# Windowed attention on one core: a PSUM copy moved from ScalarE to VectorE, and a group of transposes moved between the two halves of the score matmuls

## The chip, the cores and the metric

The kernel runs on one core of a Trainium2 chip. A core has a matmul engine (TensorE, PE in the profile, its weight loads PEld), VectorE (DVE), ScalarE (ACT), GpSimd (POOL) and SyncE (SP), each with its own instruction stream; they meet at semaphores. The metric is the device time of one execution in microseconds (us).

## What is computed

Four blocks follow each other on a tensor of 16 images of 28 x 28 positions and 32 channels. The change lies in the first one, attention inside windows of 7 x 7 positions with 4 heads of 8 channels:

```python
win = win.reshape(-1, WS * WS, C)              # windows of 49 positions
qkv = win @ w_qkv + b_qkv
attn = softmax(einsum('whnd,whmd->whnm', q, k) * scale)
out = einsum('whnm,whmd->whnd', attn, v)
out = out @ w_proj + b_proj                    # x = x + out
```

The others (a convolution with a state-space scan, a triangle product, a gated recurrence) are the same in both kernels.

## The kernel before

The partitions hold 4 groups of 32 channels (`G = 4`, group g of images on partitions 32g to 32g+31), and the columns are cut into `NS = 16` strips of 196, each one row of four windows for every group. Each engine has a function for one stage `s` (`pe_att`, `act_att`, `dve_att`, `pool_att`), and stage s works on three strips at once: it prepares strip s+1 (`nxt`: queries, keys, values), takes the scores and their exponentials of strip s (`cur`), turns the probabilities of strip s-1 and multiplies them with the values (`prv`), and projects strip s-2 (`prv2`). The order of work on each engine is written out by hand; there is no scheduler. The stages from 3 on run in loops of two stages on PE, ACT, DVE and POOL.

In one stage PE does, in this order:

- `transposes(0)`: the probabilities `Pr` of group 0 of strip s-1, four transposes of 113 x 113 (L1167), into one of two PSUM banks that the four groups take by turns (`pair2` and `pair3`, the "ring").
- `scores(0)` and `scores(1)` (L1127): queries times keys, groups 0 and 1, then groups 2 and 3. Each matmul has 32 rows of weights and 64 columns, so it sits in one of eight tiles of the array: the row of tiles is the group, and the column is the half of the output's partitions. A half of the scores is eight matmuls of 196 columns; the line has x32 in the profile, two records for a matmul. Semaphore `s_r` counts the halves.
- `transposes(1)`, then queries and keys of strip s+1 (L1203, L1204) into `banks[4]`, then `transposes(2)` and `transposes(3)`.
- `project()` (L1149) writes the projection into the same `banks[4]`, so it waits until ACT has taken queries and keys from it (`k_r`); it also waits for the attended values `AO` from DVE (`ao_r`).
- values of strip s+1 (L1221), then `av()`: probabilities times values (L1178, x64) and the sums of the softmax (L1186, x16).

ACT takes the four turned groups out of PSUM (`turned_out`, L688, `PT<-pair`), after the second of them `Qw` and `Ks` (L705, L710), then four exponentials (L697), four copies of the values (L729) and the inverse of the sums (L738, L740, tile `den`). Semaphore `ring_r` counts its copies out of the ring.

DVE takes maxima and differences of a half (`shifted`, L1851 and L1857, two each), then `AO` (L1863), then the other half, then the residual `X` (L1880). Between stages it has other small work to do, such as the normalization of a later image.

```python
                shifted(0)
                if prv2:
                    attended()
                shifted(1)
```

Of the kernel before, what the change touches and what calls it, by code (L numbers as in the profile page):

```python
# [14 lines left out]
G = P // C  # L15
# [6 lines left out]
WT = WS * WS  # L22
# [19 lines left out]
def build(nc, a, out):  # L42
    ctx = ExitStack()
    with ctx:
# [164 lines left out]

        qk_d, v_r, s_r, t_r, av_r, pj_r, q_r, k_r, exp_r, ring_r = sems("qk_d v_r s_r t_r av_r pj_r q_r k_r exp_r ring_r")
        xw_r, km_r, max_r, sub_r, sum_r, ln_r, rec_r, ao_r, x1_r, ones_r = sems("xw_r km_r max_r sub_r sum_r ln_r rec_r ao_r x1_r ones_r")


# [428 lines left out]
        def _(eng):  # L644
# [31 lines left out]
            def act_att(s, par, before_output=None):  # L676
                fixed = isinstance(s, int)
                nxt = not fixed or s + 1 < NS
                cur = not fixed or 0 <= s < NS
                prv = not fixed or 1 <= s <= NS  # L680
                np_ = 1 - par
                def turned_out(g):
                    if not prv:
                        return
                    eng.wait_ge(t_r, 4 * (s - 1) + g + 1)
                    if g == 0 and (not fixed or s >= 2):
                        eng.wait_ge(sum_r, s - 1)
                    eng.activation(PT[0:KW, g].rearrange("p a b (o q) -> p (a b o) q", o=2),  # L688
                                   banks[5 + (par + 1 + g) % 2][0:KW, :].rearrange("p (m k) -> p m k", k=WP)[:, :, 0:WT], ACT.Copy).then_inc(ring_r, 1)

                def exponent(g):
                    if not cur:
                        return
                    eng.wait_ge(sub_r, 4 * s + g + 1)
                    if not fixed or s >= 2:
                        eng.wait_ge(t_r, 4 * (s - 2) + g + 1)
                    eng.activation(Pr[:, par, g, :, 0:WT], Ts[:, g, :, :], ACT.Exp).then_inc(exp_r, 1)  # L697

                turned_out(0)
                turned_out(1)  # L700
                if nxt:
                    eng.wait_ge(qk_d, s + 2)
                    if not fixed or s >= 1:
                        eng.wait_ge(s_r, 2 * s)
                    eng.activation(Qw[:, np_, :, 0:WT].rearrange("p w (r c) -> p w r c", r=WS),  # L705
                                   windows(banks[4][:, 0:ST]), ACT.Identity,
                                   bias=vec[:, V_BQS:V_BQS + 1], scale=SCALE).then_inc(q_r, 1)
                    if not fixed or s >= 1:
                        eng.wait_ge(km_r, s)
                    eng.activation(Ks[:, np_].rearrange("p w (r c) -> p w r c", r=WS),  # L710
                                   windows(banks[4][:, ST:2 * ST]), ACT.Identity,
                                   bias=vec[:, V_BK:V_BK + 1]).then_inc(k_r, 1)
                turned_out(2)
                turned_out(3)
                for g in range(G):
                    exponent(g)
                if nxt:
                    eng.wait_ge(v_r, s + 2)
                    if not fixed or s >= 1:
                        eng.wait_ge(av_r, s)  # L720
                    if fixed and s < 0:
                        eng.wait_ge(s_mk2, 3)
                    vb = banks[5 + (par + 1) % 2]
                    for u in range(2):
                        for o in range(2):
                            src = vb[64 * o:64 * o + 64, 0:2 * P].rearrange("p (m e q d) -> p m e q d", m=8, e=2, q=2)[:, :, :, u, :]
                            dst = Vst[64 * u:64 * u + 64, np_, o].rearrange("p v g e n -> p (v g) (e n)")
                            dst = bass.AP(dst.tensor, dst.offset + HD * u, [list(dst.ap[0]), [64, 8], [48, 2], [1, HD]])
                            ins = eng.activation(dst, src, ACT.Copy)  # L729
                        ins.then_inc(ring_r, 1)  # L730

                if fixed and s < 0:
                    evacuated(3, 1)
                if before_output:
                    before_output()
                if prv:
                    eng.wait_ge(sum_r, s)
                    eng.activation(den[:, :], banks[7][:, 256:256 + ST], ACT.Ln).then_inc(ln_r, 1)  # L738
                    eng.wait_ge(ln_r, s)
                    eng.activation(den[:, :], den[:, :], ACT.Exp, scale=-1.0).then_inc(rec_r, 1)  # L740
# [344 lines left out]
        def _(eng):  # L1085
# [18 lines left out]
            def pe_att(s, par, early=None, late=None):  # L1104
# [45 lines left out]


                last = fixed and s == NS
                base = 6 * (s - 1) + 4 - (2 if last else 0)

                def transposes(g):
                    eng.wait_ge(exp_r, 4 * (s - 1) + g + 1)

                    if g == 0:
                        eng.wait_ge(ring_r, base if last else base - 2)
                    elif g == 1:  # L1160
                        eng.wait_ge(ring_r, base)
                    else:
                        eng.wait_ge(ring_r, base + g - 1)
                    bk = banks[5 + (par + 1 + g) % 2]
                    for k in range(4):
                        pg = Pr[0:KW, np_, g, 2 * k:2 * k + 2, :].rearrange("p h k -> p (h k)")[:, 0:KW]
                        ins = eng.transpose(bk[0:KW, P * k:P * k + KW], pg, ident[0:KW, 0:KW])  # L1167
                    ins.then_inc(t_r, 1)

                def av():  # L1170

                    eng.wait_ge(ring_r, base + G)
                    if not fixed or s >= 2:
                        eng.wait_ge(ao_r, s - 1)
                    for w in range(NW):
                        for e in range(2):
                            for g in range(G):
                                ins = eng.matmul(banks[7][C * g:C * g + C, WT * w:WT * w + WT], Vst[:, np_, w % 2, w // 2, g, e, :],  # L1178
                                                 PT[:, g, w // 2, e, WT * (w % 2):WT * (w % 2) + WT],
                                                 start=(e == 0), stop=(e == 1))  # L1180
                    ins.then_inc(av_r, 1)
                    if fixed and s == 1:
                        eng.wait_ge(ones_r, 3)
                    for e in range(2):
                        for g in range(G):
                            ins = eng.matmul(banks[7][C * g:C * g + C, 256:256 + ST], ones[:, e, :], PT[:, g, :, e, :],  # L1186
                                             start=(e == 0), stop=(e == 1))
                    ins.then_inc(sum_r, 1)
# [1 line left out]
                if prv:  # L1190
                    transposes(0)
                scores(0)
                scores(1)
                if prv:
                    transposes(1)
                if nxt:
                    if fixed and s < 1:
                        eng.wait_ge(s_xn, s + 2)
                    if not fixed or s >= 0:
                        eng.wait_ge(k_r, s + 1)  # L1200
                    if not fixed or s >= 3:
                        eng.wait_ge(x1_r, s - 2)
                    eng.matmul(banks[4][:, 0:ST], BD[:, U_Q, :], XN[:, strip(s + 1)], start=True, stop=True)  # L1203
                    eng.matmul(banks[4][:, ST:2 * ST], BD[:, U_K, :], XN[:, strip(s + 1)], start=True, stop=True).then_inc(qk_d, 1)  # L1204
# [11 lines left out]
                if nxt:  # L1216
                    eng.wait_ge(xw_r, s + 2)
                    if prv:
                        eng.wait_ge(ring_r, base + 3)
                    for v in range(NW // 2):  # L1220
                        ins = eng.matmul(banks[5 + (par + 1) % 2][:, P * v:P * v + P],  # L1221
                                         xw[:, np_, 2 * v:2 * v + 2].rearrange("p o k -> p (o k)"),
                                         BD[:, U_V, :], start=True, stop=True)
                    ins.then_inc(v_r, 1)
# [19 lines left out]
            def claim(name, b):  # L1244
# [8 lines left out]
                        eng.wait_ge(a_m, d + 1)  # L1253
                elif place(name, b) >= 2:

                    eng.wait_ge(ring_r, 6 * NS)
                    eng.wait_ge((x1_r, ao_r)[place(name, b) - 2], NS)
                order.append((name, b))

# [458 lines left out]
        def _(eng):  # L1718
# [119 lines left out]
            def dve_att(s, par, before_residual=None):  # L1838
# [21 lines left out]
                def attended():  # L1860
# [2 lines left out]
                    eng.tensor_tensor(windows(AO[:, par, :]), by_window(banks[7][:, 0:ST]),  # L1863
                                      by_window(den[:, :]), ALU.mult).then_inc(ao_r, 1)

                shifted(0)
                if prv2:
                    attended()
# [400 lines left out]
```

## Time and profile before

| what | value |
|---|---|
| median of 3 runs | 429.19 us (427.34 to 432.02) |
| the profiled execution: its own time, and its span | 428.95 us, 426.8 us |
| mean granted TensorE clock | 0.967 |
| attention's stages | about 14 to 123 us of the span |
| one stage in its steady state | 6.40 us |

The span is the time from the first to the last instruction; some 2.15 us of the execution's time lie around it. The row of each stage begins where `transposes(0)` does.

### The profile page before, as it was taken

How to read it: one execution, taken by the hardware profiler on the slowest of the kernel's cores; microseconds unless marked ns; L12 is line 12 of the kernel's file. 1: busy time of each engine (PE TensorE's matmuls, PEld its weight loads, DVE VectorE, ACT ScalarE, POOL GpSimd, SP SyncE). 2: the span in 40 equal slices, each digit the busy share in tenths (PEclk: the TensorE clock that was granted, in tenths of full speed). 3: DMA queues.
4: the chain of work that ended last, by engine and by line, in shares of the span. 5: the costliest groups of instructions: out<-in, count | busy, mean ns of one | idle time of the engine just before them, and what ended most of it. 6: DMA issues, size and time to landing. Idle time of an engine off the chain costs nothing.

```text
span 426.8 us, 11111 instructions
## 1 busy us (share of the span) xinstructions
PE 373.2 (87%) x4065; PEld 256.2 (60%) x4065; DVE 318.9 (75%) x637; ACT 286.2 (67%) x600; POOL 162.3 (38%) x139
## 2 busy tenths in 40 slices
PE   5899999999998798798799776898978979999996
PEld 5677777777754243253354333443963569888885
DVE  3879887788746699899689889995658957555554
ACT  3589899999858676649857764449974354444443
POOL 8314323223103246754954978961632400000000
PEclk9989999999999898899989988999999989999999
DMA  6120000004123353354222222200030001111111
GB/s 162 7 20 8 2 0 1 0 0 98 34 67 93 116 141 119 116 144 119 103 103 102 102 98 97 85 0 0 2 77 2 2 1 23 16 22 22 22 22 27
DMA packets 28671, 23.17 MB, mean 54 GB/s; under 512 B 21105, under 2 KB 22897, under 8 KB 28641
## 3 DMA queue, kind: packets, MB, share of 16 engines
q1 hardware_dynamic: 28244, 22.73, 19.4%
q8 instruction: 18, 0.29, 0.3%
q10 hardware_dynamic: 396, 0.05, 0.1%
q14 instruction: 13, 0.10, 0.1%
HBM read 2.00 MB, written 1.61 MB: 8 GB/s over the span
## 4 chain that ended last, share of the span: by engine, by line
PE 37%; DVE 25%; issue 13%; ACT 9%; POOL 7%; DMA 4%; SPq 3%; DVEq 1%; ACTq 0%; POOLq 0%
PE pair L1671 6%; DVE pair L1966 3%; PE pair L1291 3%; PE pair L1167 3%; DVE Ts L1857 3%; PE pair L1178 3%; DVE stats L1745 3%; PE pair L1127 3%; PE pair L1659 2%; DMA Cs<-BCf 2%; SPq L419 2%; DVE Hs L1978 2%; PE pair L1186 2%; PE pair L1149 2%; PE pair L1279 2%
## 5 line engine op out<-in xcount | busy, mean ns | idle before, releaser
L535 POOL TENSOR_TENSOR hC<-Hs,Cs 128x784 f32<-128x784 f32 x31 | 61.9, 2001 | 47.5 <-DVE Hs L1978 31.6
L503 POOL TENSOR_TENSOR Km<-Ks,mask 128x784 f32<-128x784 f32 x16 | 24.2, 1509 | 69.3 <-ACT Ks L710 69.3
L1344 PE MATMUL pair<-hC,ident 128*128 128x392 f32 x128 | 50.4, 520 | 0.0
L1851 DVE TENSOR_REDUCE mx<-pair 128x8 f32<-128x392 f32 x64 | 32.9, 555 | 17.0 <-PE pair L1127 17.0
L1340 PE MATMUL pair<-BCf,sel 96*128 96x392 bf16 x64 | 22.5, 355 | 19.9 <-DVE Hs L1978 17.6
L1966 DVE TENSOR_TENSOR pair<-DU,pair 128x392 f32<-128x392 f32 x64 | 35.5, 555 | 5.8 <-PE pair L1340 5.3
L1671 PE MATMUL pair<-hst,BD 128*128 128x112 f32 x224 | 37.2, 297 | 2.1 <-DVE Rt L2238 0.4
L1167 PE MATMUL pair<-ident,Pr 113*113 113x113 f32 x256 | 37.1, 279 | 2.1 <-issue 1.2
L1167 PEld LDWEIGHTS pair<-ident,Pr 113*113 113x113 f32 x256 | 31.0, 183 | 12.2 <-issue 11.4
L1978 DVE TENSOR_TENSOR_SCAN Hs<-dA,Hs,pair 128x392 f32<-128x392 f32 x32 | 32.9, 1030 | 3.3
L1671 PEld LDWEIGHTS pair<-hst,BD 128*128 128x128 f32 x224 | 29.6, 192 | 9.1 <-DVE hst L2232 5.2
L1978 DVE TENSOR_TENSOR_SCAN Hs<-dA,pair 128x392 f32<-128x392 f32 x32 | 31.1, 970 | 4.2
L1344 PEld LDWEIGHTS pair<-hC,ident 128*128 128x128 f32 x128 | 25.0, 200 | 15.2 <-issue 5.2
L827 ACT ACTIVATE dA<-DL,Aneg 128x784 f32<-128x784 f32 x32 | 29.1, 941 | 6.8 <-POOL DL L545 5.3
L1659 PE MATMUL pair<-XN,BD 128*128 (+1 forms) x224 | 31.7, 286 | 1.8 <-ACT XN L1048 1.8
L697 ACT ACTIVATE Pr<-Ts 128x392 f32<-128x392 f32 x64 | 31.4, 546 | 2.5 <-DVE Ts L1857 1.9
L1857 DVE TENSOR_TENSOR Ts<-pair,mx 128x392 f32<-128x392 f32 x64 | 32.8, 553 | 0.0
L1340 PEld LDWEIGHTS pair<-BCf,sel 96*128 96x128 bf16 x64 | 6.3, 100 | 43.4 <-issue 37.5
L688 ACT ACTIVATE PT<-pair 113x392 f32<-113x392 f32 x64 | 29.7, 496 | 3.9 <-PE pair L1167 2.9
L1659 PEld LDWEIGHTS pair<-XN,BD 128*128 128x128 f32 x224 | 28.0, 197 | 2.3 <-ACT XN L1048 2.3
L1068 ACT ACTIVATE gates<-pair 128x112 f32<-128x112 f32 x28 | 7.4, 264 | 28.9 <-PE pair L1671 28.9
L2219 DVE SCALAR_TENSOR_TENSOR prods<-gates 128x112 f32<-128x112 f32 x28 | 7.7, 275 | 24.0 <-ACT gates L1068 24.0
(255 smaller groups left out, 851.2 us busy)
## 6 DMA issues: line engine op xcount, KB each, us to landing
Cs<-BCf SPq DMA_DIRECT2D x32, 392.0 KB
SX<-XP SPq DMA_DIRECT2D x48, 112.2 KB
XT<-in_x SPq DMA_DIRECT2D x4, 392.0 KB, 6.4
out<-Os SPq DMA_DIRECT2D x28, 56.0 KB, 1.7
AD<-Aa SPq DMA_DIRECT2D x4, 196.0 KB
NB<-in_L_conv_x_proj_w SPq DMA_DIRECT2D x4, 3.0 KB
DW<-in_L_conv_dw SPq DMA_DIRECT2D x4, 1.1 KB
W<-in_L_conv_w_qkv ACTq DMA_DIRECT2D x1, 48.0 KB
```

Source lines behind the costliest of these rows:

```text
L535: eng.tensor_tensor(hC[:, i % NHC, :], Hs[:, i % NHS, :], Cs[i % NCS][:, :], ALU.mult).then_inc(v_c, 1)
L688: eng.activation(PT[0:KW, g].rearrange("p a b (o q) -> p (a b o) q", o=2), banks[5 + (par + 1 + g) % 2][0:KW, :].rearrange("p (m k) -> p m ...
L697: eng.activation(Pr[:, par, g, :, 0:WT], Ts[:, g, :, :], ACT.Exp).then_inc(exp_r, 1)
L827: eng.activation(dA[:, n % NA, :], DL[:, c % 2, :], ACT.Exp, scale=Aneg[:, n:n + 1]).then_inc(a_da, 1)
L1167: ins = eng.transpose(bk[0:KW, P * k:P * k + KW], pg, ident[0:KW, 0:KW])
L1344: return eng.matmul(STATES[:, h, :], ident[:, :], src[:, columns(h)], start=first, stop=last)
L1659: eng.matmul(zb[k].rearrange("p (b n) -> p b n", b=J), BD[:, U_X + k, :], xt, start=False, stop=False, skip_group_check=True)
L1671: eng.matmul(zb[k], BD[:, U_M + k, :], hst[:, 1 - par, :], start=False, stop=True, skip_group_check=True).then_inc(done, 1)
L1851: eng.tensor_reduce(mx[:, g, :], banks[g][:, 0:392].rearrange("p (m k) -> p m k", k=WT), AX.X, ALU.max).then_inc(max_r, 1)
L1857: eng.tensor_tensor(Ts[:, g, :, :], banks[g][:, 0:392].rearrange("p (m k) -> p m k", k=WT), bcast(mx[:, g, :], 2, WT), ALU.subtract).then_ ...
L1966: eng.tensor_tensor(SPREAD[:, columns(h)], DU[:, c % 2, columns(h)], SPREAD[:, columns(h)], ALU.mult).then_inc(v_b, 1)
L1978: eng.tensor_tensor_scan(Hs[:, i % NHS, columns(h)], dA[:, n % NA, columns(h)], SPREAD[:, columns(h)], h0, ALU.mult, ALU.add).then_inc(v_s, 1)
```

## The change

Group 0's turned probabilities are copied out of PSUM by DVE, as its first work of a stage, ahead of the maxima; the copy has a semaphore of its own, `t0_r`. ACT is left with groups 1 to 3, so `ring_r` counts 5 copies a stage where it counted 6. On PE, `transposes(1)` stands between `scores(0)` and `scores(1)`. The waits follow: `transposes(2)` waits for `t0_r` (its bank is group 0's), `transposes(3)` for ACT's copy of group 1, `av()` for both counters.

```diff
@@ act_att
-                    if g == 0 and (not fixed or s >= 2):
+                    if g == 1 and (not fixed or s >= 2):
                         eng.wait_ge(sum_r, s - 1)
...
-                turned_out(0)
                 turned_out(1)
@@ pe_att
-                base = 6 * (s - 1) + 4 - (2 if last else 0)
+                base = 5 * (s - 1) + 4 - (2 if last else 0)
...
                     elif g == 1:
                         eng.wait_ge(ring_r, base)
+                    elif g == 2:
+                        eng.wait_ge(t0_r, s)
                     else:
-                        eng.wait_ge(ring_r, base + g - 1)
+                        eng.wait_ge(ring_r, base + 1)
...
-                    eng.wait_ge(ring_r, base + G)
+                    eng.wait_ge(t0_r, s)
+                    eng.wait_ge(ring_r, base + 3)
...
                 if prv:
                     transposes(0)
                 scores(0)
-                scores(1)
                 if prv:
                     transposes(1)
+                scores(1)
...
                     if prv:
-                        eng.wait_ge(ring_r, base + 3)
+                        eng.wait_ge(ring_r, base + 2)
@@ dve_att
+                if prv:
+                    eng.wait_ge(t_r, 4 * (s - 1) + 1)
+                    if prv2:
+                        eng.wait_ge(sum_r, s - 1)
+                    eng.tensor_copy(PT[0:KW, 0].rearrange("p a b (o q) -> p (a b o) q", o=2),
+                                    banks[5 + (par + 1) % 2][0:KW, :].rearrange("p (m k) -> p m k", k=WP)[:, :, 0:WT]).then_inc(t0_r, 1)
                 shifted(0)
                 if prv2:
                     attended()
```

On PE, stage 2 before, from `transposes(0)` to the first of `transposes(2)`; `pair0` holds the scores of groups 0 and 1, `pair1` those of 2 and 3, `pair2` has `banks[4]` and one bank of the ring, `pair3` the other one:

```order
L1167 MATMUL pair3<-ident,Pr 113x113 [waits ring_r,exp_r]
L1127 MATMUL pair0<-Km,Qw 64x196 [waits sub_r,km_r,q_r]
L1127 MATMUL pair0<-Km,Qw 64x196 x7
L1127 MATMUL pair1<-Km,Qw 64x196 [waits sub_r]
L1127 MATMUL pair1<-Km,Qw 64x196 x7
L1167 MATMUL pair2<-ident,Pr 113x113 [waits ring_r,exp_r]
L1167 MATMUL pair2<-ident,Pr 113x113 x3
L1203 MATMUL pair2<-XN,BD 128x196 [waits k_r]
```

The same place now:

```order
L1168 MATMUL pair3<-ident,Pr 113x113 [waits ring_r,exp_r]
L1126 MATMUL pair0<-Km,Qw 64x196 [waits sub_r,km_r,q_r]
L1126 MATMUL pair0<-Km,Qw 64x196 x7
L1168 MATMUL pair2<-ident,Pr 113x113 [waits ring_r,exp_r]
L1168 MATMUL pair2<-ident,Pr 113x113 x3
L1126 MATMUL pair1<-Km,Qw 64x196 [waits sub_r]
L1126 MATMUL pair1<-Km,Qw 64x196 x7
L1205 MATMUL pair2<-XN,BD 128x196 [waits k_r]
L1168 MATMUL pair3<-ident,Pr 113x113 [waits t0_r,exp_r]
```

The second group's transposes stand between the two halves of the scores, and the scores of groups 2 and 3 directly ahead of the queries (L1205). On DVE, stage 5 before, after the normalization of an image:

```order
L1764 TENSOR_SCALAR XN<-X,mv,rstd 128x784 [waits s_mv,s_rs]
L1851 TENSOR_REDUCE mx<-pair0 128x8 [waits s_r]
L1857 TENSOR_TENSOR Ts<-pair0,mx 128x392 [waits exp_r,max_r] x2
L1863 TENSOR_TENSOR AO<-pair3,den 128x4x7x7 [waits rec_r]
L1851 TENSOR_REDUCE mx<-pair1 128x8 [waits s_r]
```

And now:

```order
L1767 TENSOR_SCALAR XN<-X,mv,rstd 128x784 [waits s_mv,s_rs]
L1873 COPY PT<-pair2 113x392 [waits sum_r,t_r]
L1854 TENSOR_REDUCE mx<-pair0 128x8 [waits s_r]
L1860 TENSOR_TENSOR Ts<-pair0,mx 128x392 [waits exp_r,max_r] x2
L1866 TENSOR_TENSOR AO<-pair3,den 128x4x7x7 [waits rec_r]
```

The copy stands ahead of the maxima and waits for the transposes of group 0 (`t_r`).

## Rows read from the trace of the kernel before

**Rows 1.** The chain that ended last, by engine and by line (the page).

```profile
PE 37%; DVE 25%; issue 13%; ACT 9%; POOL 7%; DMA 4%; SPq 3%; DVEq 1%; ACTq 0%; POOLq 0%
```

**Rows 2.** Timeline of stage 7: start, duration, engine, line, tiles, idle before.

```profile
60.55 1.08 DVE L1769 TENSOR_TENSOR BD<-W,bd 128x896 f32<-128x896 f32 x1
...
61.01 0.65 PE L1167 MATMUL pair<-ident,Pr 113*113 113x113 f32 x4
...
61.59 0.95 PE L1127 MATMUL pair<-Km,Qw 32*64 32x196 f32 x32
...
62.46 0.47 PEld L1167 LDWEIGHTS pair<-ident,Pr 113*113 113x113 f32 x4 [0.28 <-issue]
62.46 0.65 PE L1167 MATMUL pair<-ident,Pr 113*113 113x113 f32 x4
62.55 1.04 DVE L1851 TENSOR_REDUCE mx<-pair 128x8 f32<-128x392 f32 x2 [0.92 <-PE pair L1127]
62.67 0.97 ACT L688 ACTIVATE PT<-pair 113x392 f32<-113x392 f32 x2
...
62.95 0.51 PE L1203 MATMUL pair<-XN,BD 128*128 x2
...
63.30 0.49 PE L1204 MATMUL pair<-XN,BD 128*128 x2
...
63.63 0.96 PE L1167 MATMUL pair<-ident,Pr 113*113 113x113 f32 x8
63.91 0.43 ACT L705 ACTIVATE Qw<-pair,vec 128x196 f32<-128x196 f32 x1 [0.26 <-PE pair L1204]
64.23 0.42 ACT L710 ACTIVATE Ks<-pair,vec 128x196 f32<-128x196 f32 x1
64.45 0.35 DVE L1863 TENSOR_TENSOR AO<-pair,den 128x196 f32<-128x196 f32 x1
64.54 0.89 ACT L688 ACTIVATE PT<-pair 113x392 f32<-113x392 f32 x2
...
64.93 0.59 PE L1149 MATMUL pair<-AO,BD 128*128 128x196 f32 x2 [0.34 <-DVE AO L1863]
```

**Rows 3.** Windows: busy time of stage 7 (PE, PEld, DVE, ACT, POOL), granted clock.

```profile
61.00:67.40 6.40, 6.06 (x142) 4.98 (x138) 5.09 (x11) 5.94 (x17) 1.81 (x2) 1.00 0.00 0
```

**Rows 4.** Timeline of stage 0, where a wait parts the two halves of the scores.

```profile
15.74 0.54 PEld L1127 LDWEIGHTS pair<-Km,Qw 32*64 32x64 f32 x16 [0.43 <-ACT X L268]
...
16.57 0.60 PE L1203 MATMUL pair<-XN,BD 128*128 128x196 f32 x2
...
17.00 0.49 PE L1204 MATMUL pair<-XN,BD 128*128 128x196 f32 x2
```

**Rows 5.** Timeline of stage 2: the keys and the attended values.

```profile
31.55 0.42 ACT L710 ACTIVATE Ks<-pair,vec 128x196 f32<-128x196 f32 x1
...
31.92 0.35 DVE L1863 TENSOR_TENSOR AO<-pair,den 128x196 f32<-128x196 f32 x1
```

**Rows 6.** Timeline of stage 1, PE.

```profile
22.60 0.88 PE L1167 MATMUL pair<-ident,Pr 113*113 113x113 f32 x4 [0.79 <-ACT Vst L729]
...
23.27 0.88 PE L1203 MATMUL pair<-XN,BD 128*128 128x196 f32 x2
...
24.59 1.73 PE L1167 MATMUL pair<-ident,Pr 113*113 113x113 f32 x8
```

**Rows 7.** Windows: the same stretch of stage 1, columns as in rows 3.

```profile
22.90:26.20 3.30, 3.30 (x16) 3.14 (x14) 3.15 (x7) 2.32 (x6) 0.54 (x1) 0.50 0.22 18
```

**Rows 8.** A DVE copy out of PSUM ahead of the stages (timeline).

```profile
14.34 0.97 DVE L268 COPY X<-pair 128x448 f32<-128x448 f32 x1 [0.77 <-PE pair L1095]
```

**Rows 9.** Waits from 28 to 115 us: total, times, longest.

```profile
DVE mx L1851 <- PE pair L1127: 17.0, 11, 2.0
```

**Rows 10.** Timeline of stage 15, which has no queries and keys.

```profile
113.77 1.95 PE L1167 MATMUL pair<-ident,Pr 113*113 113x113 f32 x12
...
115.75 0.35 DVE L1863 TENSOR_TENSOR AO<-pair,den 128x196 f32<-128x196 f32 x1
```

More of the change, by code:

```diff
@@ L206, in sems @@
             return [sem(n) for n in names.split()]
-        qk_d, v_r, s_r, t_r, av_r, pj_r, q_r, k_r, exp_r, ring_r = sems("qk_d v_r s_r t_r av_r pj_r q_r k_r exp_r ring_r")
+        qk_d, v_r, s_r, t_r, av_r, pj_r, q_r, k_r, exp_r, ring_r, t0_r = sems("qk_d v_r s_r t_r av_r pj_r q_r k_r exp_r ring_r t0_r")
         xw_r, km_r, max_r, sub_r, sum_r, ln_r, rec_r, ao_r, x1_r, ones_r = sems("xw_r km_r max_r sub_r sum_r ln_r rec_r ao_r x1_r ones_r")
@@ L1254, in claim @@
                 elif place(name, b) >= 2:
-                    eng.wait_ge(ring_r, 6 * NS)
+                    eng.wait_ge(ring_r, 5 * NS)
+                    eng.wait_ge(t0_r, NS)
                     eng.wait_ge((x1_r, ao_r)[place(name, b) - 2], NS)
```

## The prediction

> **What bounds the kernel now.** I read three views in this order: the chain that ended last, the timeline of one steady stage, and the windows for the busy time in it. In the chain PE leads with 37%, DVE follows with 25% and ACT has 9% [rows 1]; the reader is to see that work alternates between PE and DVE and that ACT's copies are hardly on it. The timeline of stage 7 shows the loop [rows 2]. PE turns group 0 from 61.01, runs all scores from 61.59; DVE, idle for 0.92 us, begins the maxima of groups 0 and 1 at 62.55, takes two maxima and two differences and then `AO`, done at 64.45 + 0.35 = 64.80; the projection begins at 64.93, and then values, probabilities times values and sums lead to the next `transposes(0)`, one stage of 6.40 us later. So what ends the projection's wait is `AO`. Right behind it is a second path to the same projection: scores, `transposes(1)`, queries (62.95), keys (63.30), ACT's `Qw` (63.91) and `Ks` (done at 64.23 + 0.42 = 64.65). It is 0.15 us early. In stage 2 it is 32.27 - 31.97 = 0.30 us early [rows 5]. I take 0.20 us as the slack of the keys' path in a stage. PE is busy for 6.06 of 6.40 us and ACT for 5.94, so neither can take much more [rows 3].
>
> **The copy on DVE.** DVE gains one copy of 113 x 392 out of PSUM a stage. The trace has no such copy. The nearest rows are the maximum over 392 columns of PSUM, 1.04 us for two that overlap a little, some 0.55 us each [rows 2], and a copy of 128 x 448 out of PSUM with scattered writes, 0.97 us [rows 8]. ACT's own copy of the same tile is 0.97 us for two [rows 2]. I take 0.55 us. It may begin when group 0 is turned, 61.01 + 0.65 = 61.66, and DVE waits for the scores until 62.55 anyway; in stage 7 it has even finished an extra product at 60.55 + 1.08 = 61.63. So it ends near 62.25, and the maxima keep their start. This gap is DVE's wait for the scores, 17.0 us in 11 waits between 28 and 115 us, the longest 2.0 [rows 9]. At 0.97 us the copy would end near 62.65 and put `AO` 0.1 us later; where DVE comes late from its extra work, by up to 0.55 to 0.97 us. I set it at nothing, since the path by way of the keys becomes later still (below), by about 0.75 us a stage. If that cover were gone, a late stage would pay up to 0.55.
>
> **The copy off ACT.** ACT loses 0.45 to 0.5 us a stage, between `den` and the copy of group 1. What follows is `Qw`, and before it ACT already sits idle for 0.26 us, waiting for the keys' matmul [rows 2]. Group 1's copy can't begin before its transposes end, now near 62.42 + 0.65 = 63.07 (below), so it ends near 63.6 as before, ahead of `Qw`: zero on the path.
>
> **The transposes between the halves.** This is the term that counts. Before, both halves of the scores together hold PE from 61.59 to 62.46, 0.87 us [rows 2]. Stage 0 shows what one half alone takes: the weight loads of the second half begin at 15.74, after a wait that parts them from the first, and the query matmul begins at 16.57 [rows 4]. That is 0.83 us for 8 matmuls against 0.87 for 16. The halves lie in different rows of tiles of the array, and run at the same time when they are issued one behind the other. A group of transposes uses 113 rows and columns, so with `transposes(1)` between them the halves are run one after the other, and the second costs its full time again.
>
> Step by step in stage 7: `scores(0)` from 61.59, 0.83 us; `transposes(1)`, 0.58 us (from `transposes(0)` at 61.01 to the scores at 61.59); `scores(1)`, 0.83; and from the first query matmul to the first key matmul 0.43, as in stage 0 behind scores (16.57 to 17.00), where it is 0.35 behind transposes. The keys' matmul then begins at 61.59 + 0.83 + 0.58 + 0.83 + 0.43 = 64.26 in place of 63.30, 0.96 us later. `Qw` and `Ks` follow it at once and end 0.96 us later, at 65.61. The projection needs both `Ks` and `AO`; `AO` stays, so 0.20 us of slack is used up and the projection is 0.76 us later. `transposes(2)` and `(3)` end near 65.55, before it. What stands behind the projection (values, probabilities times values, sums, next `transposes(0)`) moves with it, as do ACT's two last copies. The second half of the maxima comes behind `AO` and still finds its scores done, near 63.8.
>
> Bounds of this term: no less than if a half cost half of the pair, 0.44 us. Then the keys' matmul begins at 61.59 + 0.44 + 0.58 + 0.44 + 0.43 = 63.48, 0.18 later, inside the slack: 0. No more than if each half takes the pair's 0.87 and no slack is left: 1.04 us. I take 0.76, because stage 0 measures the very thing, with the same operands and the query matmul behind it.
>
> The Trainium skill says the same of the array (TensorEngine Tiling (Array Packing), Key Properties): tiles run in parallel, and changing the tiling mode drains the engine. The trace agrees, with 0.28 us of idle weight loading ahead of the transposes after the scores [rows 2]. By its rule of independent tiles alone a half would cost as much as the pair, 0.87 us, an estimate of 1.04 a stage before slack and of 441 us in all.
>
> **How many stages.** Queries and keys are made behind the scores in stages 1 to 14. Stages 2 to 14 are 13: 13 x 0.76 = 9.9 us. Stage 1 has no `AO`, and its path runs through PE: `transposes(1)` wait there for ACT's values and start at 22.60, with the queries at 23.27 [rows 6]. Now `scores(1)` comes behind them, at least 0.83 us. TensorE's granted clock is 0.50 there, the lower of its two levels (1.2 of 2.4 GHz) [rows 7], so it may be up to 1.6; what comes later then leaves the slow stretch, in which eight transposes took 1.73 us instead of 0.96. I take 1.0. Stage 15 has no queries: its 12 transposes, begun at 113.77, are done at 115.72, before `AO` at 116.10 [rows 10], and a second half of scores ahead of the last 8 leaves the projection waiting on `AO` or a copy at nearly the same time: 0, at most 0.2. Stages 16 and 17 have no scores; DVE's copy there lies in a long wait: 0.
>
> Sum: 9.9 + 1.0 = 10.9 us. The profiled execution's 428.95 becomes 439.9, its span 437.7; the median of the runs, 429.19, lies 0.24 above the profiled one and becomes 440.1. I forecast 440.0.
>
> **Rivals.**
>
> *The halves cost only their share* (a half 0.44 us). Then the keys' path stays within its slack, stages 2 to 14 pay nothing and stage 1 about 0.5: 429.7 us. For it: 16 matmuls in eight tiles could have been serial in part. Against it: rows 4, the only place where a half stands alone. Chance 0.06.
>
> *Part of it only.* Stage 0's 0.83 us may hold an unseen wait that a steady stage lacks. With 0.66 us a half the keys' matmul is 0.62 later, 13 x 0.42 + 0.8 = 6.3 us: 435.5. Chance 0.08.
>
> *ACT is the bound, and the change is faster.* ACT is busy for 5.94 of 6.40 us [rows 3], and four copies, a `Qw` and a `Ks` stand in a row between `den` and the projection. If ACT's length set the stage, the 0.49 us taken from it would shorten each stage until PE's 6.06 us bind: 0.34 x 13 = 4.4 us, 424.8. It decides where ACT never waits between `den` and `Ks`. Against it: the 0.26 us that ACT waits for PE before `Qw` [rows 2]. It needs the halves to cost nothing as well. Chance 0.03. The Trainium skill speaks for this side (TensorEngine Tiling (Array Packing), PSUM Bottleneck): once tiling has sped up TensorE the PSUM copies may bind, and both ScalarE and VectorE should take them out. The row on `Qw` says that they don't bind here.
>
> *DVE's copy lands on the path as well.* If it takes 0.97 us and all 13 stages start their maxima 0.5 us late or more, `AO` still ends near 65.3, before the new `Ks` at 65.6; only three or four stages with extra DVE work would pay some 0.3 us each: 441. Were it to cost more than 1.3 us, it would pass the keys: 443 to 445. Chance 0.03.
>
> **How the numbers follow.** The forecast has 0.80, and its own spread (0.6 to 0.95 us a stage, 0.8 to 1.6 in stage 1) is 437.5 to 443. A measurement of this kernel tells about 1%, 4.3 us, from no change. The range reaches down to the partial case and up to each half at the pair's price: 434.5 to 443.5, which leaves out the first and the third rival and part of the last. Slower by over 1% are the forecast, the partial case and the copy on the path, 0.91, less 0.02 for the partial case's lower edge: 0.89. Within 1%: 0.08. Faster: 0.03.
>
> **What would show it.** In the profile of the changed kernel a steady stage should be near 7.15 us long. The score matmuls should come as two groups of x16, 1.4 us apart, each 0.83 us from the next full-array matmul. The projection's wait should end by ACT's `Ks` instead of `AO`. ACT should wait about 1.2 us ahead of `Qw`, and DVE's copy should start right behind group 0's transposes and end before the scores. I am wrong if the query matmul follows the second half after 0.5 us or less, if the projection still waits for `AO`, or if the copy takes over 1 us.

## The result, and the profile after

The changed kernel takes 442.02 us (median of 4 runs, 439.73 to 443.77) beside 430.39 us for the kernel before (4 runs): a ratio of 1.0268, with a 95% interval of 1.0219 to 1.0317. It is slower by 11.6 us. The forecast was 440.0 us, and slower.

The profiled execution took 443.5 us with a span of 441.3 us, one of the longer of the four; the rows below are from it. First the chain that ended last, by engine and by line, from its page:

```profile
PE 42%; DVE 21%; issue 11%; ACT 10%; POOL 7%; DMA 6%; ACTq 1%; SPq 1%; DVEq 1%; POOLq 0%
PE pair L1168 6%; PE pair L1126 6%; PE pair L1674 5%; DVE pair L1975 4%; DMA Cs<-BCf 3%; PE pair L1180 3%; PE pair L1294 3%; PE pair L1188 2%; DVE Hs L1987 2%; DVE stats L1748 2%; PE pair L1148 2%; PE pair L1205 2%; PE pair L1223 2%; POOL hC L535 2%; DMA vec<-in_L_conv_b_qkv 2%
```

PE had 37% of the chain and DVE 25% [rows 1]; now PE has 42 and DVE 21. The transposes (L1168) and the scores (L1126) lead it.

The timeline of stage 7, which answers to [rows 2] (start, duration, engine, line, tiles, idle before):

```profile
67.27 0.65 PE L1168 MATMUL pair<-ident,Pr 113*113 113x113 f32 x4
...
67.85 0.89 PE L1126 MATMUL pair<-Km,Qw 32*64 32x196 f32 x16
67.96 0.57 DVE L1873 COPY PT<-pair 113x392 f32<-113x392 f32 x1 [0.65 <-PE pair L1168]
...
68.67 0.65 PE L1168 MATMUL pair<-ident,Pr 113*113 113x113 f32 x4
68.81 1.04 DVE L1854 TENSOR_REDUCE mx<-pair 128x8 f32<-128x392 f32 x2 [0.28 <-PE pair L1126]
...
69.25 0.89 PE L1126 MATMUL pair<-Km,Qw 32*64 32x196 f32 x16
...
70.07 0.30 PEld L1205 LDWEIGHTS pair<-XN,BD 128*128 128x128 f32 x2 [0.28 <-issue]
...
70.51 0.49 PE L1206 MATMUL pair<-XN,BD 128*128 x2
...
70.71 0.35 DVE L1866 TENSOR_TENSOR AO<-pair,den 128x196 f32<-128x196 f32 x1
...
71.12 0.43 ACT L704 ACTIVATE Qw<-pair,vec 128x196 f32<-128x196 f32 x1 [1.27 <-PE pair L1206]
71.45 0.42 ACT L709 ACTIVATE Ks<-pair,vec 128x196 f32<-128x196 f32 x1
...
71.91 0.30 PEld L1148 LDWEIGHTS pair<-AO,BD 128*128 128x128 f32 x2 [0.30 <-ACT Ks L709]
...
74.45 0.65 PE L1168 MATMUL pair<-ident,Pr 113*113 113x113 f32 x4
```

What the reader is to see: the scores are two rows of x16 where they were one of x32. From the start of the first half (67.85) to the transposes is 0.82 us, and from the start of the second (69.25) to the queries 0.82 us, where both halves together took 0.87. The keys' matmul starts 3.24 us after the stage did (67.27 to 70.51); it was 2.29 us (61.01 to 63.30). `AO` is done 3.79 us after the stage's start, exactly as before (67.27 to 71.06, and 61.01 to 64.80), but `Ks` only at 71.87, and that is what the projection now waits for. The stage is 7.18 us long in place of 6.40. PE's own work has become nearly as long as that path: `transposes(2)` and `(3)` end at 71.79 (70.84 + 0.95), 0.12 us ahead of the projection, where they ended 0.34 us ahead before (63.63 + 0.96 = 64.59, and 64.93).

The windows of that stage and of one near the end (us, then PE, PEld, DVE, ACT, POOL busy, and the granted clock), which answer to [rows 3]:

```profile
67.27:74.45 7.18, 7.06 (x143) 5.44 (x139) 5.08 (x12) 5.36 (x16) 2.08 (x3) 1.00 0.00 0
110.20:117.30 7.10, 7.06 (x143) 5.49 (x139) 5.18 (x12) 5.35 (x16) 1.82 (x2) 1.00 0.72 163
```

PE is busy for 7.06 of the 7.18 us, 1.0 more than before with the same work (142 and 143 records). ACT is busy for 5.36 in place of 5.94.

The increments of `s_r`, by which PE tells DVE of each half, show the same thing: in stage 7 the two come 0.16 us apart before (62.52 and 62.68), and 1.41 us apart now (68.78 and 70.19). Before, the two halves ran side by side and ended together.

Over stages 2 to 14 the starts of `transposes(0)` give 93.28 us (31.10 to 124.38) where they gave 83.90 (28.41 to 112.31): 9.4 us more, 0.72 a stage.

Stage 1, PE (timeline) and then the granted clock from 22.9 to 26.2 and from 26.3 to 29.7 us (windows), which answer to [rows 6, 7]:

```profile
22.85 1.07 PE L1168 MATMUL pair<-ident,Pr 113*113 113x113 f32 x4 [1.69 <-ACT Vst L728]
...
23.85 1.58 PE L1126 MATMUL pair<-Km,Qw 32*64 32x196 f32 x16
...
25.36 1.02 PE L1205 MATMUL pair<-XN,BD 128*128 128x196 f32 x2
...
26.83 1.73 PE L1168 MATMUL pair<-ident,Pr 113*113 113x113 f32 x8
...
29.59 0.91 PE L1180 MATMUL pair<-PT,Vst 128*32 128x49 f32 x64
```

```profile
22.90:26.20 3.30, 3.30 (x23) 2.38 (x24) 2.90 (x6) 0.83 (x3) 0.00 (x0) 0.50 0.23 16
26.30:29.70 3.40, 3.40 (x23) 3.00 (x25) 3.37 (x8) 2.34 (x6) 1.81 (x2) 0.51 0.18 29
```

At the lower level (0.50 of full, 1.2 GHz) the second half of the scores takes 1.51 us to the queries (23.85 to 25.36). The low stretch goes on to about 29.7 us here, where it ended near 26.2 before. `av()` begins at 29.59; in the kernel before it began at 26.91:

```profile
26.91 0.91 PE L1178 MATMUL pair<-PT,Vst 128*32 128x49 f32 x64
```

### The profile page after: what moved, and what is told of

Its sections match the earlier page's. It is cut to its first block, busy times and chain, and to the rows that moved or that the text cites. A ratio compares the mean times of both kernels' runs of the same rounds, so it can differ in the third digit from the quotient of the medians.

```text
span 441.3 us, 11123 instructions
## 1 busy us (share of the span) xinstructions
PE 387.3 (88%) x4065; PEld 262.3 (59%) x4065; DVE 326.7 (74%) x653; ACT 277.9 (63%) x584; POOL 164.9 (37%) x139
## 4 chain that ended last, share of the span: by engine, by line
PE 42%; DVE 21%; issue 11%; ACT 10%; POOL 7%; DMA 6%; ACTq 1%; SPq 1%; DVEq 1%; POOLq 0%
PE pair L1168 6%; PE pair L1126 6%; PE pair L1674 5%; DVE pair L1975 4%; DMA Cs<-BCf 3%; PE pair L1180 3%; PE pair L1294 3%; PE pair L1188 2%; DVE Hs L1987 2%; DVE stats L1748 2%; PE pair L1148 2%; PE pair L1205 2%; PE pair L1223 2%; POOL hC L535 2%; DMA vec<-in_L_conv_b_qkv 2%
## 5 line engine op out<-in xcount | busy, mean ns | idle before, releaser
L1347 PE MATMUL pair<-hC,ident 128*128 128x392 f32 x128 | 48.5, 502 | 0.0
L1343 PE MATMUL pair<-BCf,sel 96*128 96x392 bf16 x64 | 22.3, 351 | 20.5 <-DVE Hs L1987 16.6
L1168 PE MATMUL pair<-ident,Pr 113*113 113x113 f32 x256 | 37.1, 280 | 2.9 <-ACT Vst L728 1.7
L1168 PEld LDWEIGHTS pair<-ident,Pr 113*113 113x113 f32 x256 | 31.2, 184 | 13.0 <-issue 12.2
L697 ACT ACTIVATE Pr<-Ts 128x392 f32<-128x392 f32 x64 | 29.4, 551 | 1.1 <-DVE Ts L1860 1.1
L1126 PE MATMUL pair<-Km,Qw 32*64 32x196 f32 x512 | 29.2, 343 | 0.3 <-issue 0.2
L688 ACT ACTIVATE PT<-pair 113x392 f32<-113x392 f32 x48 | 22.2, 500 | 10.3 <-PE pair L1168 10.3
```

The costliest lines, as they stand in the source:

```text
L1126: ins = eng.matmul(banks[g][64 * half:64 * half + 64, 196 * pair:196 * pair + 196], Qw[C * g:C * g + C, par, 2 * pair + half, :], Km[C * g ...
L1347: return eng.matmul(STATES[:, h, :], ident[:, :], src[:, columns(h)], start=first, stop=last)
```

## The experiments

All are timed against the kernel before on the same chip as they were.

**Only the copy on DVE.** The changed kernel with PE's old order:

```diff
                 scores(0)
+                scores(1)
                 if prv:
                     transposes(1)
-                scores(1)
```

> Group 0's copy on DVE ahead of the maxima as in the changed kernel, but transposes(1) behind both halves of the scores as before. Theory (the split of the scores carries the whole loss): the copy, 0.57 us, fits between group 0's transposes and the first scores, a steady stage stays at 6.40 us, the maxima start late only in the three or four stages with extra DVE work; 430 to 431 us beside 430 before, a ratio of 1.000 to 1.003. Rival (the copy on DVE is a good part of the 12 us): 433 us or more, with steady stages of 6.6 us or more.

Measured: 432.19 us (12 runs) beside 430.63 (23 runs), ratio 1.0031, interval 0.9996 to 1.0066. That is 1.3 us by the ratio and 1.6 between the medians; the median lies 1.2 us above the end of what was expected, and the interval (-0.2 to 2.8 us) excludes neither nothing nor the lower edge of the rival (433 us). What speaks against the rival is the steady stage, 6.40 us long, in which the copy is free. This is stage 7 of its profile (timeline):

```profile
63.06 0.65 PE L1168 MATMUL pair<-ident,Pr 113*113 113x113 f32 x4
63.64 0.95 PE L1126 MATMUL pair<-Km,Qw 32*64 32x196 f32 x32
63.75 0.57 DVE L1873 COPY PT<-pair 113x392 f32<-113x392 f32 x1
...
64.60 1.04 DVE L1854 TENSOR_REDUCE mx<-pair 128x8 f32<-128x392 f32 x2 [0.29 <-PE pair L1126]
```

The copy ends at 64.32 and the maxima begin 1.54 us after the stage did, as before (61.01 to 62.55 in [rows 2]). But where DVE has extra work the copy comes on top. Stage 4 of the same profile:

```profile
43.77 1.03 PE L1126 MATMUL pair<-Km,Qw 32*64 32x196 f32 x32
...
44.54 0.24 DVE L1810 TENSOR_SCALAR TB<-TB,omean 128x32 f32<-128x32 f32 x1
...
44.81 0.57 DVE L1873 COPY PT<-pair 113x392 f32<-113x392 f32 x1
...
45.30 1.03 DVE L1854 TENSOR_REDUCE mx<-pair 128x8 f32<-128x392 f32 x2
...
47.67 0.59 PE L1148 MATMUL pair<-AO,BD 128*128 128x196 f32 x2 [0.82 <-DVE AO L1866]
```

DVE is free only at 44.78, the copy starts then, and PE waits 0.82 us for `AO`. This stage is 6.95 us long (43.19 to 50.14); the same stage of the kernel before took 6.57 (41.52 to 48.09), and its projection waited for `Ks` and not for `AO`. By the same starts the copy costs 0.26 us in stage 3, 0.38 in stage 4 and 0.48 in stage 11, and 1.16 us over stages 2 to 14 (85.06 for 83.90). So the cover that the prediction named (the later keys) is needed in some stages.

**Only the order on PE.** The kernel before with `transposes(1)` between the halves; four copies on ACT:

```diff
                 scores(0)
-                scores(1)
                 if prv:
                     transposes(1)
+                scores(1)
```

> Only transposes(1) between the halves of the scores; all four copies stay on ACT. Theory: the whole loss, 441 to 442.5 us, with steady stages of 7.1 to 7.2 us whose projection waits for the keys. Rival (the copy shares in the loss, or taking it off ACT hides a part): under 438 or over 445 us.

Measured: 441.42 us (4 runs) beside 430.63, ratio 1.0249, interval 1.0190 to 1.0308. This one edit carries the whole loss, as far as can be measured. The window of one stage (7.2 us wide, a little over the stage; columns as above) reads

```profile
67.40:74.60 7.20, 7.08 (x142) 5.44 (x138) 4.58 (x11) 5.79 (x17) 2.14 (x3) 1.00 0.00 0
```

with `transposes(0)` at 67.48 and again at 74.66, a stage of 7.18 us. ACT's copy of group 0 is back (5.79 us busy for 5.36), and the stage is no longer for it: ACT waits 1.27 us for the keys' matmul ahead of `Qw`, as in the changed kernel. The copy on DVE makes no measurable difference to the loss, and in the traces almost none: stages 2 to 14 take 93.11 us here and 93.28 in the changed kernel.

**One transpose between the halves.** The second argument names the transposes of the group that are run (the edit inside `transposes` is left out here).

```diff
                 scores(0)
+                if prv:
+                    transposes(1, (0,))
                 scores(1)
                 if prv:
-                    transposes(1)
+                    transposes(1, (1, 2, 3))
```

> The kernel before with one of the four transposes of group 1 between the halves of the scores, the other three behind the second half. Theory (what costs is that the halves don't run side by side; anything that uses the whole array between them parts them): nearly the full loss, steady stages of 7.0 to 7.4 us, 439 to 444 us. Rival (the loss goes with how much is put between them): a quarter of it, 433 us.

Measured: 440.48 us (4 runs), ratio 1.0229, interval 1.0170 to 1.0287. A quarter of what was put between costs as much as all of it. PE in one stage of its profile (timeline):

```profile
66.57 0.65 PE L1170 MATMUL pair<-ident,Pr 113*113 113x113 f32 x4
67.15 0.89 PE L1127 MATMUL pair<-Km,Qw 32*64 32x196 f32 x16
67.97 0.35 PE L1170 MATMUL pair<-ident,Pr 113*113 113x113 f32 x1
68.26 0.89 PE L1127 MATMUL pair<-Km,Qw 32*64 32x196 f32 x16
69.08 0.55 PE L1170 MATMUL pair<-ident,Pr 113*113 113x113 f32 x3
...
73.75 0.45 PE L1170 MATMUL pair<-ident,Pr 113*113 113x113 f32 x2
```

Each half again holds PE for 0.82 us (67.15 to 67.97, 68.26 to 69.08), and the stage is 7.18 us (66.57 to 73.75). In these two kernels what costs is that the halves are parted, not by how much.

**The halves cut another way.** Is it that a half uses four tiles of eight, or does any group of scores that stands alone pay 0.8 us? The changed kernel, with the scores halved by pairs of windows, so that each half of 8 matmuls sits in all eight tiles:

```diff
-                        eng.wait_ge(sub_r, 4 * s - 2 + 2 * part)
+                        eng.wait_ge(sub_r, 4 * s)
...
-                    for pair in range(NW // 2):
+                    for pair in (part,):
                         for e in range(2):
-                            for g in (2 * part, 2 * part + 1):
+                            for g in range(G):
@@ shifted
-                    eng.wait_ge(s_r, 2 * s + part + 1)
+                    eng.wait_ge(s_r, 2 * s + 2)
```

> The changed kernel, but the scores are halved by window pairs in place of groups: each half is one pair of windows of all four groups, so its 8 matmuls sit in all eight tiles of the array; the maxima wait for both halves. Theory (a half of two groups costs almost as much as both because it uses four tiles of eight): from the start of a half to the next matmul that uses the whole array it is some 0.5 us in place of 0.82, and the keys are ready 0.6 to 0.7 us earlier in a stage than in the changed kernel. AO comes 0.75 us later, since the maxima now wait for the second half, and takes over the projection's wait: stages of 7.0 to 7.2 us again, 439 to 443 us. Rival (each half pays a fixed price for being alone, such as the change of mode, whatever its tiles): 0.82 us from a half to the next matmul as before, stages of 7.4 us or more, over 444 us.

Measured: 444.14 us (4 runs) beside 430.24, ratio 1.0305, interval 1.0259 to 1.0351: 1.1 us above the end of the forecast, and by the time alone in the rival's range (over 444). So the time does not decide here; the rows do. Stage 7 of its profile (timeline):

```profile
67.43 0.65 PE L1169 MATMUL pair<-ident,Pr 113*113 113x113 f32 x4
...
68.01 0.59 PE L1127 MATMUL pair<-Km,Qw 32*64 32x196 f32 x16
...
68.52 0.65 PE L1169 MATMUL pair<-ident,Pr 113*113 113x113 f32 x4
...
69.10 0.59 PE L1127 MATMUL pair<-Km,Qw 32*64 32x196 f32 x16
...
69.62 0.60 PE L1206 MATMUL pair<-XN,BD 128*128 x2
69.80 1.04 DVE L1855 TENSOR_REDUCE mx<-pair 128x8 f32<-128x392 f32 x2 [1.12 <-PE pair L1127]
...
72.18 0.59 PE L1149 MATMUL pair<-AO,BD 128*128 128x196 f32 x2 [0.83 <-DVE AO L1867]
...
74.65 0.65 PE L1169 MATMUL pair<-ident,Pr 113*113 113x113 f32 x4
```

The same 8 matmuls hold PE for 0.51 and 0.52 us (68.01 to 68.52, 69.10 to 69.62) where they held it for 0.82. So the price of a parted half is that of its tiles: two matmuls behind each other in each of four tiles, beside one in each of eight. The rival of a fixed price of 0.8 us falls. The 0.31 us between the two is about the length of one matmul's record (0.32 us); an estimate from these numbers is that some 0.2 us of each parted group do not depend on how its tiles are filled. The stage is 7.22 us long, as forecast, and for the reason that was forecast: the maxima wait for the second half, and the projection for `AO` again. What the time has above the forecast lies in part outside the steady stages: the queries of stage 0 come 0.5 us later than before (17.08 for 16.57), and from the start of stage 15 to `av()` of stage 16 it is 18.61 us where it was 17.78.

**Stage 1 alone.** `transposes(1)` between the halves in stage 1, all other stages as before:

```diff
                 scores(0)
+                if prv and fixed and s == 1:
+                    transposes(1)
                 scores(1)
-                if prv:
+                if prv and not (fixed and s == 1):
                     transposes(1)
```

> The kernel before with transposes(1) between the halves of the scores in stage 1 alone. In the changed kernel's profile stage 1 lost 2.4 us where 1.0 was forecast, and TensorE's low clock lasted from 22.8 to 29.6 us in it, where it ended at 26.2 before. Theory (the split itself costs 1.5 us there, at the low clock, and the longer low stretch the rest): 1.5 to 2.6 us more than before, 432 to 433 us. Rival (the 2.4 us are mostly the clock's own course in one execution, which differs between executions of any kernel): 1 us or less, 430 to 431.5 us.

Measured: 431.77 us (12 runs) beside 430.24 (17 runs), ratio 1.0030, interval 1.0000 to 1.0060: 1.3 us by the ratio, at most 2.6. This lies between the two ranges, and the times don't decide between the two theories. Its profile shows the second half at 23.79 and the queries at 25.31, so 1.5 us at the low clock, and again a low stretch longer than before. But the low clock's stretch is long in the profile of the kernel with only the copy, too, which leaves PE's order alone:

```profile
22.15:28.90 6.75, 6.10 (x76) 5.74 (x80) 5.81 (x18) 4.87 (x13) 1.81 (x2) 0.50 0.22 22
```

So its length in one profile can't be laid to the split. The profiles can be compared stage by stage, though. In the kernel with only the copy the queries of stage 0 and `av()` of stage 1 begin at (timeline)

```profile
16.77 0.60 PE L1205 MATMUL pair<-XN,BD 128*128 128x196 f32 x2
...
27.76 1.40 PE L1180 MATMUL pair<-PT,Vst 128*32 128x49 f32 x64
```

10.99 us apart, with a long low stretch and no split. Before, with a short one, it is 10.34 us (16.57 to 26.91). With the split it is 12.77 in the changed kernel (16.82 to 29.59), 12.77 with only the order (16.55 to 29.32) and 12.69 with stage 1 alone (16.85 to 29.54). So in these profiles the long low stretch costs some 0.65 us and the split some 1.75 more; there is one profile of each kernel.

**Both halves first.** The two paths to the projection suggest the opposite move: scores ahead of both groups of transposes, all else as before.

```diff
-                if prv:
-                    transposes(0)
                 scores(0)
                 scores(1)
                 if prv:
+                    transposes(0)
                     transposes(1)
```

> The kernel before with both halves of the scores ahead of transposes(0) and (1), so that DVE's maxima start 0.58 us earlier in a stage. Theory (two paths end at the projection, AO's some 0.2 us behind that of the keys): AO's path is shortened by 0.58 us, the keys' path is unchanged and takes over, a stage of 6.2 to 6.25 us; 13 x 0.2 = 2.6 us faster, 427 to 428 us beside 430. Rival (AO's path alone sets the stage): 5.8 us a stage, 423 us. Rival (the stage is set elsewhere, by PE or ACT): 430 us.

Measured: 427.01 us (12 runs, 425.99 to 427.97) beside 430.63, ratio 0.9915, interval 0.9887 to 0.9944. It is faster than both kernels, by 3.6 us than the one before, and within the forecast. Its stage 7 (timeline):

```profile
61.09 0.94 PE L1127 MATMUL pair<-Km,Qw 32*64 32x196 f32 x32
...
61.97 1.04 PE L1167 MATMUL pair<-ident,Pr 113*113 113x113 f32 x8
...
62.85 0.51 PE L1202 MATMUL pair<-XN,BD 128*128 x2
...
63.95 0.35 DVE L1862 TENSOR_TENSOR AO<-pair,den 128x196 f32<-128x196 f32 x1
64.13 0.42 ACT L710 ACTIVATE Ks<-pair,vec 128x196 f32<-128x196 f32 x1
...
64.60 0.30 PEld L1149 LDWEIGHTS pair<-AO,BD 128*128 128x128 f32 x2 [0.30 <-ACT Ks L710]
...
67.13 0.61 PE L1127 MATMUL pair<-Km,Qw 32*64 32x196 f32 x16
```

`AO` is ready at 64.30 and `Ks` at 64.55, so the keys' path has taken over, as forecast. The stage is 6.04 us (61.09 to 67.13), shorter than the 6.2 expected, because that path became shorter too: from the stage's start to the queries it is 1.76 us (61.09 to 62.85), where it was 1.94 (61.01 to 62.95 in [rows 2]) with the same matmuls. The two groups of transposes now follow each other (x8, 1.04 us), and between the sums and the queries PE changes between tiles and the whole array once, where it changed there, back and there again. That this is what saves the 0.18 us was not tested by itself. A stall ate part of the gain in one stage: 1.12 us inside the scores of stage 4, with no semaphore to wait for.

```profile
43.36 0.19 PEld L1127 LDWEIGHTS pair<-Km,Qw 32*64 32x64 f32 x2 [1.12 <-issue]
```

Its cause is open. The kernel before has a smaller one at the same place: its scores of stage 4 take 1.22 us to the transposes (42.10 to 43.32), and 0.87 in stage 7.

## Why the prediction was right

**What bounds the kernel.** Right. `AO` ended the projection's wait and the keys were just behind it. Delaying the keys alone (only the order) made them the bound; bringing `AO` earlier (both halves first) did too. What the account left out is a third term, PE's own order of work: it read PE's 6.06 busy us of 6.40 as near the limit and put `transposes(3)` 0.06 us ahead of `Ks`, but did not price it. In the changed kernel PE is busy for 7.06 of 7.18 us and those transposes end 0.12 us ahead of the projection, so the keys' path and PE's work end the wait almost together.

**The copy on DVE: nothing, with the later keys as cover.** Right in the changed kernel: 0.57 us in the trace for a forecast 0.55, done at 68.53, before the maxima at 68.81. Against the kernel with only the order changed it makes no difference that can be measured (ratios 1.0268 and 1.0249). The cover mattered: with it gone, the copy cost 1.3 us in all (-0.2 to 2.8), in stages with extra DVE work.

**The copy off ACT: nothing.** Right. ACT's wait before `Qw` grew from 0.26 to 1.27 us, and with only the copy moved the steady stage stayed at 6.40 us.

**The transposes between the halves: 0.76 us a stage.** Right, and it carries the result. The terms were 0.83, 0.58, 0.83 and 0.43 us; the trace has 0.82, 0.58, 0.82 and 0.44. The keys' matmul is 0.95 us later for a forecast 0.96, and the stage 0.78 us longer in its steady form (7.18 to 6.40) and 0.70 near the end (7.10, with 6.40 before). Over the 13 stages it is 9.4 us for a forecast 9.9, 0.72 a stage. The row of stage 0 was the right one to size it by; the transposes in between and the tiles were then each tested by a kernel of their own.

**The number of stages, 13.** Right; stage 15 cost nothing in the profile: from its predecessor's probabilities times values to its own are 6.12 us after (122.89 to 129.01) and 6.13 before.

**Stage 1: 1.0 us.** Mis-sized in the profiled execution. There the start of `av()` moved from 26.91 to 29.59, 2.68 us, of which 0.25 lies ahead of the attention stages. The split half took 1.51 us at the low clock, near the upper bound given (1.6), and the low stretch did not end where it ended before, which the working had counted on. Without the 0.25 it is 2.4 us for a forecast 1.0. The profile of the kernel with only the copy has as long a low stretch and loses 0.65 us, so the split itself accounts for some 1.75. Over many runs the stage alone costs 1.3 us (0 to 2.6), so what it costs in a usual execution stays open.

The sum was 10.9 us and the measured difference is 11.6. That they are so near is in part luck: in the profile the 13 stages came out 0.5 below their term and stage 1 came out 1.4 above. The profiled span grew by 14.5 us; about 12 of it are there when the last of attention's `av()` begins (142.16 after, 130.09 before). The rest, some 2.4, lies behind the attention, where the kernels are the same, and no run here explains it; the other three runs of the changed kernel have spans of 437.6, 438.4 and 441.6 us.

The rivals: that the halves cost only their share is refuted by each 0.82 us; the partial case too; that ACT is the bound is refuted by the kernel with only the copy, in which ACT has a copy less and nothing gets shorter. (The prediction's reading for this rival, that four copies stand between `den` and the projection, is not what its rows show: two copies, `Qw` and `Ks` stand there, and the other two copies begin at 64.54 and are still running when the projection begins.) The copy as a second loss is refuted by the kernel with only the order, which loses as much.

## What to carry to other kernels

In these traces small matmuls in different tiles of the array ran side by side only where they were issued one behind the other: before moving anything between two such groups, look for a place in the trace where one group stands alone, and take its time, not half of the pair's. When two paths end at the same wait, price both from the timeline before moving work: delaying the one that is 0.2 us early costs all but 0.2 us, and shortening the last gains only until the other takes over. Add up the engine's own row as a further path: here PE, busy for 6.06 us of 6.40, had no room for one more microsecond. An engine relieved of work gains nothing where the row after it shows a wait for another engine.

## What the runs showed of the hardware

- Eight matmuls of 32 x 64 weights and 196 float32 columns hold the array for 0.82 us in four tiles, 0.51 us in eight; sixteen in eight tiles take 0.87 us.
- Two halves of eight matmuls in different rows of tiles, issued one behind the other, signalled their ends 0.16 us apart; with transposes between them 1.41 us apart.
- One 113 x 113 transpose between two groups in different tiles parts them as fully as four do (7.18 us a stage with either).
- TensorE's granted clock fell to 0.50 (1.2 GHz) between 20.5 and 23 us, at the start of the attention, for some 3.4 us (before), 6.8 us (changed, only the copy) or 10.2 us (only the order). PE had waited 0.79 us for ACT ahead of 22.60 in the kernel before, 1.69 us ahead of 22.85 in the changed one. With one profile of each kernel the runs don't show what sets the length.
- Eight 113 x 113 transposes took 1.73 us at the lower clock, 0.96 us at the full one.
- VectorE's copy of 113 x 392 float32 out of PSUM took 0.57 us, ScalarE's copy of the same tile 0.50 us.
